# Gated cross-attention block: ScalarE scales x in place, VectorE adds the mix from PSUM, start-up loads and engine orders laid out anew

## The chip, the cores and the metric

The kernel runs on one core of one Trainium2 chip. The metric is device time in microseconds; lower is better. Before the change it is 1412.2 us, the median of three runs.

## The reference

All data are float32, and the batch has 8 samples `x[b]` of 512 rows (features) by 2048 columns. Cut to what matters:

```python
# layernorm over the 2048 columns; then windowed attention in patches of W=128 columns, 8 heads of 32 rows
q = Wq @ z + bq;  k = Wk @ z + bk;  v = Wv @ ctx + bv         # z = layernorm(x), 256 x 512 weights
s = where(mask, q.T k / sqrt(32), -1e9);  a = softmax(s)
o = gelu(a v);    x = x + tanh(g_x) * mask * (Wo @ o + bo)
# second half: a row of 2048 is one token, 64 experts with a bias of 2048 each
h = layernorm(x); p = softmax(h @ Wr.T + rb);  w = top 8 of p, all others 0
x = x + tanh(g_f) * (h * sum(w) + w @ expert_bias)
```

With `h = (x - m) * r` the last line is `x * A + B + M`: per row A = 1 + tanh(g_f) * sum(w) * r and B = -tanh(g_f) * sum(w) * r * m, while M = tanh(g_f) * (w @ expert_bias) is the mix, a matrix product.

## The kernel before

**Tiling.** A sample is a batch of the loop; it lies in SBUF as `X[b % 2]`, 4 tiles `t` of 128 rows by 2048 columns. The attention works on units of 256 columns (two windows), 8 per batch, 64 in all, numbered u. The second half runs once per batch, when unit 8b+7 is done.

**Order.** There is no planner at run time. Each engine has its own instruction stream, which the Python program writes by walking over `TICKS`; `SLOTS` gives each step a lag in slots, a unit is due every 16 slots and a batch every 128. Slots are only an order: an engine issues what is next and waits on semaphores. The steps of one unit, in the order of TensorE: `S` (scores for the maximum), `DEN`, `PV` and `R0`, `R1` of older units, `q`, `v0`, `k` projections of the next unit, `MT`, `hT0`, `hT1`, `v1`, `ST` (scores turned), `WO0`, `WO1`. Products are made of a high and a low part in fp32r, so every operand has a `_hi` written by ScalarE and a `_lo` written by GpSimd or VectorE.

**PSUM.** Seven banks form a ring (`take`): at each step of the order the bank that by the slots comes free first is taken, with the semaphore of its last reader. TensorE waits for that reader.

**The batch's end.** For batch b: `norm2` (statistics), `L` (ScalarE copies the logits), `LT` (TensorE), `c_top`, `c_exp`, `c_w` (softmax and the top 8, on VectorE and ScalarE; the last step signals `ac_v` and leaves A in `sc[:, t, 6:7]` and B in `sc[:, t, 7:8]`), `wT` (TensorE), `wt_hi`, `wt_lo`, and then 16 chunks of 512 columns: `mix` (TensorE, L463 and L464), `shift_mix` (ScalarE, L684: `xm` = mix + B, PSUM to SBUF, two buffers `xm`), `add_mix` (VectorE, L879: X = X * A + `xm`), and a store of the chunk. Between the chunks stand steps of the units that run on: `ST`, `WO0`, `WO1` and `S` on TensorE, `exp` on ScalarE, `xt0`, `xt1` (`weigh_out`, L784), `top` (L747) and `rc` (reciprocal, L768) on VectorE. GpSimd adds `xt` to X (`add_x`, L1025) meanwhile.

**Statistics of the next batch** (`input_stats`, `bn1`, L887) are 16 instructions on VectorE, from slot 64.75 of a batch with a gap of 1.25 slots. The statistics of the second norm (`stats2`, `bn2`, L793) are 4 instructions in every second unit.

**Start-up.** SyncE issues all loads: six small constants, x of batch 0 as 4 loads of 1 MB, two broadcast masks, Wq, Wk, Wv, the mask table, context, Wo, router and expert weights. VectorE waits for the constants (L904), makes the selection tiles, does the 16 statistics (L887), then the splits of Wq and Wk. ScalarE waits for Wv and copies it (L689), then `z_hi` (L603). GpSimd normalises unit 0 (`z_full`, L1001) and makes `z_lo` (L1009). Then TensorE starts. At tick `SPLIT` the splits of Wo, router and expert weights stand in the streams, and behind them on VectorE the first `k_ev` (L737).

Of the kernel before, what the change touches and what calls it, by code (L numbers as in the profile page):

```python
# [27 lines left out]
def bf16_parts(v):  # L28
# [15 lines left out]
    rows=-10.75, z32=-26, z_hi=-16.75, z_lo=-14.25, q=-11, q_ev=-9, k=-9, k_ev=-3.75, mk=-33.5, mkb=-25,  # L44

    c_hi=-15, c_lo=-10.5, v=-10.5, v_ev=-7.25, v_gap=-0.75,

    S=0.75, top=2.5, split=6, MT=9, mt_ev=8.75, ST=14.25, exp=16.5, DEN=18.25, PV=18.5, rc=19, on=21.25,

    gelu=24.25, mg=5, ot_hi=24.75, ot_lo=29, WO=30.25, WO_gap=1.5, xt=32.25, x1=35.5, bn2=40,  # L50

    h=39.5, hT=43.25, hT_gap=0.25, ht_hi=45.25, ht_lo=44.75, R=51.25,
# [12 lines left out]
V_BQ, V_SUM, V_PICK, V_ROWS, V_SEL, V_ONES3, V_IDB = 2, 4, 6, 10, 12, 13, 14  # L65
# [3 lines left out]
def gated_block_kernel(nc, x, ctx, mask, g_x, g_f, wqT, wkT, wvT, woT, bq, bk, bv, bo, wrT, rb, eb, out):  # L69
    with ExitStack() as st:  # L70
# [9 lines left out]
        def f32(ap):  # L80
# [66 lines left out]
        xm = [sb(f"xm{i}", [128, 512]) for i in range(2)]  # L147
        onef = xm[0][:, 0:128]
# [44 lines left out]
        wm_v, wT_pe, wthi_a, wtlo_v, mix_pe, xm_a, x2_v = (sem(n) for n in (  # L193
            "wm", "wT", "wthi", "wtlo", "mix", "xm", "x2"))
# [70 lines left out]
        def _(e):  # L265
# [22 lines left out]
            def v_mm(p):  # L288
# [3 lines left out]
                if p == 0:  # L292
                    e.wait_ge(v_w, 5)
# [90 lines left out]
            def project_out(u, j):  # L384
# [3 lines left out]
                if u == 0 and j == 0:  # L388
                    e.wait_ge(v_w, 7)
# [61 lines left out]
            def mix(b, t, c):  # L451
# [55 lines left out]
        def _(e):  # L507
# [60 lines left out]
            e.wait_ge(v_m, V_KEEP)  # L568
            e.dma_start(rows_d.rearrange("k p i -> p k i"), keep).then_inc(sm_rowsd, 16)
            for t in TICKS:  # L570
# [27 lines left out]
        def _(e):  # L598
# [90 lines left out]
            e.activation(wv_hi[:], wvst, ACT.Copy).then_inc(a_w, 1)  # L689
            for t in TICKS:  # L690
                if t == SPLIT:
                    e.wait_ge(v_w, 6)
# [32 lines left out]
                for i in range(16):  # L725
                    for b in batch(t, C["m_ev"] + C["m_gap"] * i):
                        shift_mix(b, i // 4, i % 4)

        @block.vector
        def _(e):  # L730
# [202 lines left out]
            e.tensor_tensor(wv_lo[:], wvst, f32(wv_hi[:]), ALU.subtract).then_inc(v_w, 1)
# [3 lines left out]
            for k, part in enumerate(bf16_parts(BIG)):  # L937
                e.tensor_scalar(keep[:, k, :], mneg, part, None, ALU.mult).then_inc(v_m, 1)
            for t in TICKS:
                if t == SPLIT:  # L940
# [10 lines left out]
                    e.wait_ge(a_w, 4)  # L951
# [41 lines left out]
        def _(e):  # L993
            def z_full(u):
# [3 lines left out]
                if u:  # L998
                    e.wait_ge(zlo_g, u)
# [115 lines left out]
```

## Time and profile before

| | |
|---|---|
| median of 3 runs | 1412.2 us (1408.51 to 1414.26) |
| profiled execution, its own time | 1407.94 us |
| its span, first to last instruction | 1406.1 us |
| granted TensorE clock, mean | 0.997 |
| busy: TensorE / VectorE / ScalarE / GpSimd | 92% / 77% / 56% / 72% |
| DMA queues | 28.7% of 16 engines, 89 GB/s |

Busy shares are averages over 64 units, 8 batch ends, the start and the tail. A matmul's duration overlaps with the next one's, so that an interval fully covered by matmuls reads as busy 20.00 of 20 us.

### The profile page before, as it was taken

Reading aid. Unit: us, or ns where it says so; the run is one execution under the profiler, and the core shown is the slowest. Engines: PE = TensorE matmul, PEld = TensorE weight load, DVE = VectorE, ACT = ScalarE, POOL = GpSimd, SP = SyncE. Lnnn points to the kernel's source line nnn. Section 1 sums busy time; section 2 is a strip of 40 time slices with the busy share of each in tenths; the row PEclk is TensorE's granted clock in tenths of the full one; section 3 lists DMA queues with packets and bytes.
Section 4 is the critical chain, followed back from the end, with each engine's and each line's share of the span. In section 5 each row is a group of like instructions: output and inputs, shape, how many; then the busy total and the mean of one; then the engine's idle time right before and its main releaser. Section 6 shows DMA issues by size and latency. Waiting matters only on the chain.

```text
span 1406.1 us, 39921 instructions
## 1 busy us (share of the span) xinstructions
PE 1300.1 (92%) x16139; PEld 1162.6 (83%) x16139; DVE 1089.4 (77%) x1949; ACT 794.1 (56%) x1430; POOL 1015.5 (72%) x988
## 2 busy tenths in 40 slices
PE   1899999899989999899998999989998999989996
PEld 1898998789977899789986899878998789978974
DVE  5468678897688867898778967889668886788666
ACT  1356655655565665655556665565556565565544
POOL 4487888578866788578885688857886678857751
PEclk9999999999999999999999999999999999999999
DMA  8331111541126211361113511154111621132003
GB/s 252 112 110 41 44 46 43 167 139 46 47 62 223 64 45 48 106 201 40 48 47 125 178 43 48 43 162 140 48 48 57 217 72 47 47 98 91 27 5 120
DMA packets 129270, 124.68 MB, mean 89 GB/s; under 512 B 12352, under 2 KB 97472, under 8 KB 128448
## 3 DMA queue, kind: packets, MB, share of 16 engines
q1 hardware_dynamic: 129088, 122.14, 28.7%
q8 instruction: 129, 2.11, 0.6%
q14 instruction: 53, 0.43, 0.1%
HBM read 88.45 MB, written 33.65 MB: 87 GB/s over the span
## 4 chain that ended last, share of the span: by engine, by line
PE 67%; DVE 20%; ACT 5%; issue 4%; DMA 2%; POOL 1%; SPq 1%; DVEq 0%; ACTq 0%; POOLq 0%
PE ring L283 7%; PE ring L284 7%; PE ring L285 7%; DVE X L879 4%; PE ring L399 4%; PE ring L358 4%; PE ring L323 4%; DVE o L768 4%; PE ring L400 4%; PE ring L401 4%; PE ring L298 3%; PE ring L299 3%; PE ring L300 3%; PE ring L367 3%; PE ring L414 3%
## 5 line engine op out<-in xcount | busy, mean ns | idle before, releaser
L283 PE MATMUL ring<-z_hi,wqk_hi 128*128 128x256 f32 x1024 | 291.3, 284 | 31.2 <-POOL z_lo L1009 31.2
L284 PE MATMUL ring<-z_hi,wqk_lo 128*128 128x256 f32 x1024 | 290.3, 283 | 0.0
L285 PE MATMUL ring<-z_lo,wqk_hi 128*128 128x256 f32 x1024 | 290.1, 283 | 0.0
L1025 POOL TENSOR_TENSOR X<-X,xt 128x512 f32<-128x512 f32 x128 | 165.9, 1300 | 141.4 <-DVE xt L784 136.3
L1041 POOL TENSOR_SCALAR hc<-X,ln 128x256 f32<-128x256 f32 x256 | 234.1, 930 | 0.5 <-POOL X L1025 0.5
L784 DVE SCALAR_TENSOR_TENSOR xt<-ring,cst,mg 128x256 f32<-128x256 f32 x256 | 112.0, 479 | 146.9 <-PE ring L401 146.9
L611 ACT ACTIVATE q<-ring,cst 128x256 f32<-128x256 f32 x64 | 30.3, 474 | 346.1 <-PE ring L285 346.1
L283 PEld LDWEIGHTS ring<-z_hi,wqk_hi 128*128 128x128 f32 x1024 | 196.8, 192 | 34.3 <-issue 31.8
L768 DVE RECIPROCAL o<-ring 128x512 f32<-128x512 f32 x64 | 214.2, 3347 | 0.2 <-PE ring L367 0.2
L1015 POOL TENSOR_TENSOR cx_lo<-cx,cx_hi 128x512 fp32r<-128x512 f32 x128 | 169.0, 1320 | 46.3 <-ACT cx_hi L619 46.3
L284 PEld LDWEIGHTS ring<-z_hi,wqk_lo 128*128 128x128 f32 x1024 | 196.8, 192 | 2.5
L285 PEld LDWEIGHTS ring<-z_lo,wqk_hi 128*128 128x128 f32 x1024 | 196.9, 192 | 0.0
L747 DVE TENSOR_REDUCE mx<-ring 128x4 f32<-128x512 f32 x256 | 158.8, 682 | 32.4 <-PE ring L323 32.3
L1009 POOL TENSOR_TENSOR z_lo<-z,z_hi 128x1024 fp32r<-128x1024 f32 x64 | 152.3, 2380 | 43.1 <-ACT z_hi L603 43.1
L399 PE MATMUL ring<-ot_hi,wo_hi 128*128 128x256 f32 x512 | 151.7, 296 | 6.7 <-ACT xm L684 5.9
L298 PE MATMUL ring<-wv_hi,cx_hi 128*128 128x256 f32 x512 | 149.7, 292 | 0.0
L1029 POOL TENSOR_TENSOR ot_lo<-o,ot_hi 128x512 fp32r<-128x512 f32 x64 | 83.1, 1299 | 89.7 <-ACT ot_hi L650 89.7
L1001 POOL TENSOR_SCALAR z<-X,ln 128x256 f32<-128x256 f32 x256 | 146.5, 585 | 0.1
L299 PE MATMUL ring<-wv_lo,cx_hi 128*128 128x256 f32 x512 | 144.5, 282 | 0.0
L400 PE MATMUL ring<-ot_hi,wo_lo 128*128 128x256 f32 x512 | 144.4, 282 | 0.0
L300 PE MATMUL ring<-wv_hi,cx_lo 128*128 128x256 f32 x512 | 144.3, 282 | 0.0
L401 PE MATMUL ring<-ot_lo,wo_hi 128*128 128x256 f32 x512 | 143.8, 281 | 0.0
(133 smaller groups left out, 3377.3 us busy)
## 6 DMA issues: line engine op xcount, KB each, us to landing
cx<-in_ctx SPq DMA_DIRECT2D x128, 256.0 KB, 2.8
out_y<-X SPq DMA_DIRECT2D x128, 256.0 KB, 2.7
X<-in_x SPq DMA_DIRECT2D x112, 256.0 KB, 5.8
mk<-in_mask SPq DMA_DIRECT2D x64, 128.0 KB, 3.2
mg<-in_mask SPq DMA_DIRECT2D x64, 128.0 KB, 3.2
X<-in_x SPq DMA_DIRECT2D x4, 1024.0 KB, 8.1
sel<-rows_d SPq DMA_DIRECT2D x256, 3.0 KB
X<-in_eb SPq DMA_DIRECT2D x2, 512.0 KB, 8.2
```

The lines of the kernel that those rows point to most:

```text
L283: e.matmul(o, wqk_hi[:, t, cols], z_hi[:, t, :], t == 0, False)
L284: e.matmul(o, wqk_lo[:, t, cols], z_hi[:, t, :], False, False)
L285: last = e.matmul(o, wqk_hi[:, t, cols], z_lo[:, t, :], False, t == DT - 1)
L298: e.matmul(o, cx_hi[:, k, :], wv_hi[:, k, :], k == 0, False)
L299: e.matmul(o, cx_hi[:, k, :], wv_lo[:, k, :], False, False)
L300: last = e.matmul(o, cx_lo[:, k, :], wv_hi[:, k, :], False, k == DT - 1)
L399: e.matmul(o, wo_hi[:, m, cols], ot_hi[:, m, :], m == 0, False)
L400: e.matmul(o, wo_lo[:, m, cols], ot_hi[:, m, :], False, False)
L401: last = e.matmul(o, wo_hi[:, m, cols], ot_lo[:, m, :], False, m == 1)
L768: e.reciprocal(o32[u % NO][:], bank("DEN", u)[:].rearrange("p (m i) -> p m i", m=2)).then_inc(rc_v, 1)
L1015: e.tensor_tensor(cx_lo[:], cx[p % NC][:], f32(cx_hi[:]), ALU.subtract).then_inc(cxlo_g, 1)
L1041: last = e.tensor_scalar(hc[u % 2][:, t, :], X[b % 2][:, t, c * U:(c + 1) * U], ln1[b % 2][:, 0, t:t + 1], None, ALU.add)
```

## The change

1. `shift_mix` and the buffers `xm` go. ScalarE gets `scale_x(b, t)`: X = X * A + B in place, one instruction of 128x2048 for each of the 4 row tiles, after `ac_v` and `h_g`. VectorE's `add_mix` becomes a `tensor_tensor` add of the mix in PSUM to X, 16 per batch as before. A mix bank is now freed by VectorE (`x2_v`) and no longer by ScalarE (`xm_a`).
2. Start-up: the mask table and x (8 loads of 512 KB, with an own semaphore `x_half` for first halves) are issued first; Wq and Wk go ahead of the broadcast masks; the six constants are issued by ScalarE's queue. ScalarE makes the high parts of Wq, Wk and Wv. VectorE normalises unit 0 and makes its `z_lo`; the mask preparation stands ahead of the statistics.
3. `SLOTS` is changed in most entries. In the stream of a unit the order on each engine stays as it was (but `mk` stands ahead of `ctx1` and `rows` ahead of `mg` in SyncE's). At the batch's end: `wT` behind `hT0`, `q_ev` ahead of `c_exp`, `ht_hi0` ahead of `wt_hi`; `scale_x` of tiles 0 and 1 stands ahead of `z_hi`, `v_ev1` and `exp`, tile 2 behind `exp`, tile 3 behind `c_hi0`. TensorE has mix 0 to 2, `ST`, mix 3 and 4, `WO0`, mix 5 to 10, `WO1`, mix 11 and 12, `S`, mix 13 to 15 (before: 0 to 3, `ST`, `WO0`, 4 to 9, `WO1`, 10 to 13, `S`, 14 and 15). The 16 statistics of the next batch start at slot 67.75 with a gap of 1.75.

```diff
-    S=0.75, top=2.5, split=6, MT=9, mt_ev=8.75, ST=14.25, exp=16.5, DEN=18.25, PV=18.5, rc=19, on=21.25,
+    S=0.5, top=2.75, split=5.75, MT=7.5, mt_ev=9, ST=14, exp=16.25, DEN=18.25, PV=19.25, rc=19, on=21,
-    norm2=29.5, L=34.75, LT=35.5, c_top=35, c_exp=36, c_w=42, wT=41.75, wt_hi=43.75, wt_lo=42.75, mix=45.25, m_gap=0.25,
-    m_ev=47.5, x2=47.25, rl=52.5, rl_gap=1,
+    norm2=29.5, L=33.75, LT=35.5, c_top=36, c_exp=35.5, c_w=41.5, wT=43.25, wt_hi=43.75, wt_lo=42.75, mix=45.25, m_gap=0.25,
+    sx=45.5, sx_gap=1.5, x2=47.25, rl=55.5, rl_gap=1,
-    x_1=0.5, x_gap=3.75, bn1=64.75, bn1_gap=1.25, norm1=95,
+    x_1=0.5, x_gap=3.75, bn1=67.75, bn1_gap=1.75, norm1=95.75,
...
-                    take(("mix", b * 16 + i), t, C["m_ev"] - C["mix"], xm_a, b * 16 + i + 1)
+                    take(("mix", b * 16 + i), t, C["x2"] - C["mix"], x2_v, b * 16 + i + 1)
...
+            e.dma_start(mT, mflat.rearrange("b (w i) -> (b w) i", i=128)).then_inc(sm_mT, 16)
             for t in range(DT):
-                e.dma_start(X[0][:, t, :], xv[0, t]).then_inc(x_in[0][t], 16)
+                e.dma_start(X[0][:, t, 0:1024], xv[0, t, :, 0:1024]).then_inc(x_half[t], 16)
+                e.dma_start(X[0][:, t, 1024:S], xv[0, t, :, 1024:S]).then_inc(x_in[0][t], 16)
...
-            def shift_mix(b, t, c):
-                i = (b * DT + t) * 4 + c
-                if i >= 2:
-                    e.wait_ge(x2_v, i - 1)
-                e.wait_ge(mix_pe, i + 1)
-                if t == 0 and c == 0:
+            def scale_x(b, t):
+                if t == 0:
                     e.wait_ge(ac_v, b + 1)
-                e.activation(xm[i % 2][:], bank("mix", i)[:], ACT.Identity, bias=sc[:, t, 7:8]).then_inc(xm_a, 1)
+                    e.wait_ge(h_g, NU * (b + 1))
+                xs = X[b % 2][:, t, :]
+                e.activation(xs, xs, ACT.Identity, bias=sc[:, t, 7:8], scale=sc[:, t, 6:7]).then_inc(sx_a, 1)
...
+            e.wait_ge(sm_wq, 16)
+            e.activation(wqk_hi[:, :, 0:E], wst[:, :, 0:E], ACT.Copy, scale=QSCALE).then_inc(a_w, 1)
+            e.wait_ge(sm_wk, 16)
+            e.activation(wqk_hi[:, :, E:2 * E], wst[:, :, E:2 * E], ACT.Copy).then_inc(a_w, 1)
             e.wait_ge(sm_wv, 16)
             e.activation(wv_hi[:], wvst, ACT.Copy).then_inc(a_w, 1)
...
-                e.wait_ge(xm_a, i + 1)
-                e.scalar_tensor_tensor(out=xs, in0=xs, scalar=sc[:, t, 6:7], in1=xm[i % 2][:], op0=ALU.mult, op1=ALU.add).then_inc(x2_v, 1)
+                if c == 0:
+                    e.wait_ge(sx_a, b * DT + t + 1)
+                e.wait_ge(mix_pe, i + 1)
+                e.tensor_tensor(xs, xs, bank("mix", i)[:], ALU.add).then_inc(x2_v, 1)
...
+            ln = ln1[0]
+            e.wait_ge(rstd1_g, 1)
+            for t in range(DT):
+                last = e.tensor_scalar(z32[:, t, :], X[0][:, t, 0:U], ln[:, 0, t:t + 1], ln[:, 2, t:t + 1], ALU.add, ALU.mult)
+            last.then_inc(z32_g, 1)
```

## Rows read from the trace of the kernel before

**Rows 1.** Busy time by engine in 20 us; columns PE, PEld, DVE, ACT, POOL, clock, DMA.

```profile
200.00:220.00 20.00, 20.00 (x259) 18.45 (x259) 13.26 (x22) 11.61 (x22) 16.83 (x18) 1.00 0.16 42
240.00:260.00 20.00, 16.60 (x144) 13.64 (x143) 15.81 (x34) 17.97 (x33) 6.25 (x4) 1.00 0.36 120
```

**Rows 2.** Timeline of VectorE, the reciprocal of five units: start, duration.

```profile
214.34 3.35 DVE L768 RECIPROCAL o<-ring 128x512 f32<-128x512 f32 x1
...
232.85 3.35 DVE L768 RECIPROCAL o<-ring 128x512 f32<-128x512 f32 x1
...
268.83 3.34 DVE L768 RECIPROCAL o<-ring 128x512 f32<-128x512 f32 x1
...
287.41 3.35 DVE L768 RECIPROCAL o<-ring 128x512 f32<-128x512 f32 x1
...
307.27 3.35 DVE L768 RECIPROCAL o<-ring 128x512 f32<-128x512 f32 x1
```

**Rows 3.** Timeline of VectorE in an ordinary unit.

```profile
209.05 0.88 DVE L784 SCALAR_TENSOR_TENSOR xt<-ring,cst,mg 128x256 f32<-128x256 f32 x2 [2.74 <-PE ring L401]
210.46 0.88 DVE L784 SCALAR_TENSOR_TENSOR xt<-ring,cst,mg 128x256 f32<-128x256 f32 x2 [0.53 <-PE ring L401]
211.94 2.48 DVE L747 TENSOR_REDUCE mx<-ring 128x4 f32<-128x512 f32 x4 [0.60 <-PE ring L323]
```

**Rows 4.** Who waited for whom, 233 to 270 us: total, times, longest.

```profile
ACT xm L684 <- DVE X L879: 6.8, 7, 2.4
...
PE ring L463 <- DVE mx L747: 2.4, 1, 2.4
```

**Rows 5.** Groups by line, whole span: busy us, mean ns, idle before.

```profile
L879 DVE SCALAR_TENSOR_TENSOR X<-X,sc,xm 128x512 f32<-128x512 f32 x128 | 114.2, 933 | 20.2 <-ACT xm L684 18.2
L684 ACT ACTIVATE xm<-ring,sc 128x512 f32<-128x512 f32 x128 | 85.5, 696 | 52.4 <-DVE X L879 48.8 <-PE ring L464 2.2 <-issue 1.4
L657 ACT ACTIVATE ht_hi<-ring 128x512 fp32r<-128x512 f32 x128 | 69.1, 597 | 10.5 <-PE ring L414 10.5
L773 DVE TENSOR_TENSOR o<-ring,o 128x512 f32<-128x512 f32 x64 | 43.8, 685 | 3.7
L464 PE MATMUL ring<-eb,wt_lo 128*128 128x512 f32 x128 | 50.6, 395 | 0.0
L697 ACT ACTIVATE eb<-X 128x2048 fp32r<-128x2048 f32 x1 | 1.9, 1900 | 0.0
```

**Rows 6.** Timeline of VectorE and of ScalarE at the first batch's end.

```profile
246.62 1.28 DVE L812 TENSOR_TENSOR ht_lo<-ring,ht_hi 128x512 fp32r<-128x512 f32 x2
...
246.06 1.06 ACT L603 ACTIVATE z_hi<-z 128x1024 fp32r<-128x1024 f32 x1
...
252.90 2.07 ACT L638 ACTIVATE P<-ring 128x512 f32<-128x512 f32 x4
```

**Rows 7.** Timeline of the start, all engines.

```profile
3.52 2.21 SPq L554 DMA_DIRECT2D X<-in_x  x4
...
8.61 9.95 DVE L887 BATCH_NORM_STATS2 bnst<-X 128x6 f32<-128x512 f32 x16 [1.07 <-DMA X<-in_x]
...
20.72 6.77 POOL L1001 TENSOR_SCALAR z<-X,ln 128x256 f32<-128x256 f32 x4
...
23.13 1.06 ACT L689 ACTIVATE wv_hi<-X 128x1024 fp32r<-128x1024 f32 x1 [17.46 <-DMA X<-in_wvT]
...
31.21 0.55 PE L283 MATMUL ring<-z_hi,wqk_hi 128*128 128x256 f32 x1 [31.21 <-POOL z_lo L1009]
```

**Rows 8.** Statistics on VectorE between 294 and 316 us (timeline).

```profile
294.82 3.05 DVE L887 BATCH_NORM_STATS2 bnst<-X 128x6 f32<-128x512 f32 x5
...
312.96 2.46 DVE L793 BATCH_NORM_STATS2 bn<-X 128x6 f32<-128x512 f32 x4
```

**Rows 9.** Timeline of ScalarE and of VectorE in the tail.

```profile
1388.07 0.60 ACT L675 ACTIVATE wt_hi<-ring 128x512 fp32r<-128x512 f32 x1 [2.93 <-PE ring L448]
...
1391.15 11.97 DVE L879 SCALAR_TENSOR_TENSOR X<-X,sc,xm 128x512 f32<-128x512 f32 x16 [1.69 <-ACT xm L684]
```

More of the change, by code:

```diff
@@ L42 @@
 SLOTS = dict(
-    rows=-10.75, z32=-26, z_hi=-16.75, z_lo=-14.25, q=-11, q_ev=-9, k=-9, k_ev=-3.75, mk=-33.5, mkb=-25,
-    c_hi=-15, c_lo=-10.5, v=-10.5, v_ev=-7.25, v_gap=-0.75,
-    S=0.75, top=2.5, split=6, MT=9, mt_ev=8.75, ST=14.25, exp=16.5, DEN=18.25, PV=18.5, rc=19, on=21.25,
-    gelu=24.25, mg=5, ot_hi=24.75, ot_lo=29, WO=30.25, WO_gap=1.5, xt=32.25, x1=35.5, bn2=40,
-    h=39.5, hT=43.25, hT_gap=0.25, ht_hi=45.25, ht_lo=44.75, R=51.25,
-    norm2=29.5, L=34.75, LT=35.5, c_top=35, c_exp=36, c_w=42, wT=41.75, wt_hi=43.75, wt_lo=42.75, mix=45.25, m_gap=0.25,
-    m_ev=47.5, x2=47.25, rl=52.5, rl_gap=1,
-    x_1=0.5, x_gap=3.75, bn1=64.75, bn1_gap=1.25, norm1=95,
+    rows=-11.75, z32=-24.75, z_hi=-16, z_lo=-16.5, q=-11.5, q_ev=-12.5, k=-9, k_ev=-3.75, mk=-38.5, mkb=-24.25,
+    c_hi=-14.5, c_lo=-10.5, v=-10, v_ev=-7, v_gap=-1,
+    S=0.5, top=2.75, split=5.75, MT=7.5, mt_ev=9, ST=14, exp=16.25, DEN=18.25, PV=19.25, rc=19, on=21,
+    gelu=24.5, mg=5, ot_hi=25.75, ot_lo=29.25, WO=30.5, WO_gap=1.5, xt=32.5, x1=35.25, bn2=40,
+    h=40.75, hT=43.25, hT_gap=0.25, ht_hi=43.75, ht_lo=44.75, R=51.25,
+    norm2=29.5, L=33.75, LT=35.5, c_top=36, c_exp=35.5, c_w=41.5, wT=43.25, wt_hi=43.75, wt_lo=42.75, mix=45.25, m_gap=0.25,
+    sx=45.5, sx_gap=1.5, x2=47.25, rl=55.5, rl_gap=1,
+    x_1=0.5, x_gap=3.75, bn1=67.75, bn1_gap=1.75, norm1=95.75,
 )
 G_IDENT, G_MXB = 2, 8
-V_BQ, V_SUM, V_PICK, V_ROWS, V_SEL, V_ONES3, V_IDB = 2, 4, 6, 10, 12, 13, 14
+V_SUM, V_PICK, V_ROWS, V_SEL, V_ONES3, V_IDB, V_BQ = 3, 5, 9, 11, 12, 13, 14
 V_KEEP, V_SW = 4, 6
@@ L146, in gated_block_kernel @@
         wt_lo = sb("wt_lo", [128, DT, 128], F32R)
-        xm = [sb(f"xm{i}", [128, 512]) for i in range(2)]
-        onef = xm[0][:, 0:128]
+        onef = sb("onef", [128, 128])
         half = sb("half", [128, DT])
@@ L170, in gated_block_kernel @@
         mflat = mask.rearrange("b o s -> (b o) s")
-        sm_small, sm_wqk, sm_wv, sm_mT, sm_wo = (sem("w_" + n) for n in ("x", "qk", "v", "mT", "o"))
+        sm_small, sm_wq, sm_wk, sm_wv, sm_mT, sm_wo = (sem("w_" + n) for n in ("x", "q", "k", "v", "mT", "o"))
         sm_rb, sm_wr, sm_eb, sm_rowsd = (sem("w_" + n) for n in ("rb", "r", "eb", "rows"))
@@ L176, in gated_block_kernel @@
             "g_set", "v_set", "v_w", "v_m", "a_w", "a_tg", "pe_set"))
+        x_half = [sem(f"xh{t}") for t in range(DT)]
         x_in = [[sem(f"x{i}_{t}") for t in range(DT)] for i in range(2)]
@@ L192, in gated_block_kernel @@
             "L", "LT", "dm", "lg", "t8", "neg", "mr", "sel", "ex", "w2", "ac"))
-        wm_v, wT_pe, wthi_a, wtlo_v, mix_pe, xm_a, x2_v = (sem(n) for n in (
-            "wm", "wT", "wthi", "wtlo", "mix", "xm", "x2"))
+        wm_v, wT_pe, wthi_a, wtlo_v, mix_pe, sx_a, x2_v = (sem(n) for n in (
+            "wm", "wT", "wthi", "wtlo", "mix", "sx", "x2"))
         TICKS = range(-32 * 8, 8 * (128 * (NB + 1) + 96))
@@ L273, in project @@
                     e.wait_ge(freed, n)
+                if u == 0:
+                    e.wait_ge(v_w, kind + 1)
                 if kind == 0:
-                    if u == 0:
-                        e.wait_ge(v_w, 4)
                     e.wait_ge(zhi_a, u + 1)
@@ L470, in _ @@
                     for k in range(SB):
-                        last = e.matmul(PR[:, 0:NX], onef, wrst[:, k, :], k == 0, k == SB - 1)
+                        last = e.matmul(PR[:, 0:NX], onef[:], wrst[:, k, :], k == 0, k == SB - 1)
                     last.then_inc(pe_set, 1)
@@ L724, in _ @@
                     w_high(b)
-                for i in range(16):
-                    for b in batch(t, C["m_ev"] + C["m_gap"] * i):
-                        shift_mix(b, i // 4, i % 4)
+                for i in range(DT):
+                    for b in batch(t, C["sx"] + C["sx_gap"] * i):
+                        scale_x(b, i)
         @block.vector
@@ L938, in _ @@
                 e.tensor_scalar(keep[:, k, :], mneg, part, None, ALU.mult).then_inc(v_m, 1)
+            for t in range(DT):
+                for r in range(4):
+                    input_stats(0, t, r)
+            input_norm(0)
+            ln = ln1[0]
+            e.wait_ge(rstd1_g, 1)
+            for t in range(DT):
+                last = e.tensor_scalar(z32[:, t, :], X[0][:, t, 0:U], ln[:, 0, t:t + 1], ln[:, 2, t:t + 1], ALU.add, ALU.mult)
+            last.then_inc(z32_g, 1)
+            e.wait_ge(a_w, 1)
+            e.scalar_tensor_tensor(out=wqk_lo[:, :, 0:E], in0=wst[:, :, 0:E], scalar=QSCALE, in1=f32(wqk_hi[:, :, 0:E]),
+                                   op0=ALU.mult, op1=ALU.subtract).then_inc(v_w, 1)
+            e.wait_ge(zhi_a, 1)
+            e.tensor_tensor(z_lo[:], z32[:], f32(z_hi[:]), ALU.subtract).then_inc(zlo_g, 1)
+            e.wait_ge(a_w, 2)
+            e.tensor_tensor(wqk_lo[:, :, E:2 * E], wst[:, :, E:2 * E], f32(wqk_hi[:, :, E:2 * E]), ALU.subtract).then_inc(v_w, 1)
+            e.wait_ge(sm_small, 96)
+            e.tensor_scalar(cst[:, BQ:BQ + 2], cst[:, BQ:BQ + 2], QSCALE, None, ALU.mult).then_inc(v_set, 1)
+            e.wait_ge(a_w, 3)
+            e.tensor_tensor(wv_lo[:], wvst, f32(wv_hi[:]), ALU.subtract).then_inc(v_w, 1)
             for t in TICKS:
```

75 lines of the change are left out of this document (29 added, 46 removed).

## The prediction

> **What bounds the kernel now.** First the busy time by stretch. In the middle of a batch TensorE is covered 20.00 of 20 us, while VectorE has 13.26, ScalarE 11.61 and GpSimd 16.83 [rows 1]. Two reciprocals then stand 18.51 us apart (232.85 - 214.34) [rows 2]: this unit is paid for by TensorE, and its order does not change, so nothing is won there. What a batch costs beyond its eight units the reciprocals show too: the unit with the batch's end takes 35.98 us (268.83 - 232.85), 17.5 too many, and a unit soon after it takes 19.86 (307.27 - 287.41), 1.35 too many [rows 2]. At the batch's end TensorE falls to 16.60 of 20 [rows 1]; a little later it waits 2.4 us in one piece for the maximum (L747), which is queued on VectorE between the chunk adds [rows 4]. Part of the 17.5 must stay, since the mix is real work: 32 matmuls at no more than 0.395 are at most 12.6 us [rows 5]. So at least 4.9 us per end can be won. VectorE and ScalarE alternate there through two small buffers: ScalarE waited 6.8 us for the add to give `xm` back [rows 4], and the add took 0.933 us in the mean, against 0.75 in the tail (11.97 / 16), where GpSimd is still [rows 5, 9].
>
> **The start.** Before, TensorE begins at 31.21. Wv lands at 23.13, but z of unit 0 is ready only at 20.72 + 6.77 = 27.5; `z_hi` and GpSimd's `z_lo` follow [rows 7]. After: x's first issue stood at 3.52 behind six constants; with one load left ahead of it, it comes 0 to 2.9 us earlier (five sixths of 3.52); I take 2.3, since the queue does not start at zero. As many bytes lie ahead of Wv as before, so it lands at 20.8. Then ScalarE copies Wv and makes `z_hi`, both 128x1024 as L689, 1.06 each: 22.9. VectorE's `z_lo` is twice the length of a 512-column step, which costs 0.62 when chained (9.95 / 16) [rows 7]: 1.24. TensorE begins at 24.2, **7.0 us earlier**. The other path is hidden: statistics from 5.5 or so to 15.5, the norm as before 2.2 (18.56 to 20.72) [rows 7], z on VectorE 4 times between 0 and 0.685 (L773, a longer instruction) [rows 5], so by 20.4 at the latest, ahead of ScalarE's 21.8. If Wv landed no earlier the gain is 4.7; if it were early enough for z to decide, with z at about 1.3, it is 9.9. Bounds: -4.7 to -9.9. The first `k_ev` stays behind the same splits and moves along. ScalarE's six issues, the copies of Wq and Wk and the late scaling of bq lie in ScalarE's 17.46 us of waiting for Wv [rows 7]; without that cover they would cost some 4 us.
>
> **The batch's end, followed through.** TensorE's stream up to `k` and VectorE's up to `c_w` are unchanged; `wT` lets `hT0` pass while it waits for the weights. On ScalarE the same three copies (`wt_hi`, `ht_hi0`, `ht_hi1`) are done in another order, and then the first `scale_x` takes the place that `z_hi` had, at 246.1 [rows 6]. Its price: a 128x2048 instruction without pointers took 1.900 (L697), and one bias pointer costs 0.10 (L684 against L657, 0.696 - 0.597), so with scale and bias 2.1 [rows 5]. It ends at 248.2. VectorE is done with `ht_lo` at 247.90 before and about 0.5 later after, because `wt_lo` waits for the later `wt_hi` [rows 6]: 248.4. So ScalarE does not hold it. From there VectorE does 15 adds, `xt0`, `xt1` and the maximum, until the last bank that the next `q` needs is free. An add from PSUM takes 0.685 (L773) alone and 0.62 chained [rows 5, 7]: 15 x 0.62 = 9.3. With 0.88 less an overlap of 0.08 for each `xt` and 2.48 for the maximum [rows 3] that is 13.4 us. Two pauses come to it. The fourth bank of `ST` is that of chunk 0, free at 249.1. From there TensorE has the rest of `ST` (as long as `S`, 211.94 - 210.46 = 1.5), two mixes (an estimate of 0.46 each: two matmuls of 0.395 that overlap) and `WO0` (210.46 - 209.05 = 1.4) [rows 3, 5]: 253.0. VectorE is through chunk 4 at 251.5: 1.5. Chunk 8 needs `scale_x` of tile 2, behind the exponentials. These end at 254.97 as before [rows 6], since tiles 0 and 1, `z_hi` and `v_ev1` are through at 251.5, so tile 2 is ready at 256.9; VectorE, with `xt0` and chunks 5 to 7 behind it, gets there at 255.8: 1.1. Then 248.4 + 13.4 + 2.6 = 264.4, and the reciprocal follows at 264.5 against 268.83 [rows 2]: **4.3 us per end**, seven times, -30. In the last batch the tail counts (below).
>
> Bounds of this term: if the adds came to 0.933 each, as L879 does beside GpSimd [rows 5], 16 x 0.31 = 5.0 would be lost again and the end be 0.7 slower; if both pauses closed, 6.9 would be won. I take the chained row, since L773 already reads one operand from PSUM and one from SBUF beside a busy GpSimd, 0.685 in the mean of 64. One rule speaks against the move. L773's 0.685 from PSUM stands against 0.65 to 0.75 for L879 with GpSimd still [rows 5, 9]. The Trainium skill ("VectorE: DVE Perf Modes", section on the TRN2 errata) gives VectorE a fixed cost of 120 cycles for an operand from PSUM and 58 for one from SBUF, an estimate of 65 ns more for each add. By that rule a batch's adds would cost 1.0 us more and the seven ends win 23 instead of 30; by the rows the full duration is known, and the sum needs no such addition.
>
> **Statistics of the next batch.** Before, 13 of the 16 fall into one unit, 5 of them in a row from 294.82 [rows 8], with `k_ev` behind them, and the unit costs 1.35 too much [rows 2]. After, 8 fall into each of two units. The first has 5 x 0.62 = 3.1 less on VectorE and fits. The second has 5 more than before and also `bn2` with 2.46, ending at 315.4 before [rows 8]: `k_ev` behind it comes up to 3.1 us later, and I take its slack at two thirds of that, so 1.0 is lost. So **0.4 us per batch** remains of the 1.35, -3; bounds 0 to -9.5. The later loads of x (55.5 for 52.5) keep their distance to the statistics, which also move by 3 slots. In SyncE's queue `mk` now waits for `k_ev` ahead of `ctx1`; that context tile is needed a unit later, so it costs nothing, and late by more than 10 us it would hold `c_hi`.
>
> **The tail.** `wt_hi` ends at 1388.67; `scale_x` of tile 0 runs to 1390.8, and the adds follow at 0.62: the last ends at 1390.8 + 9.9 = 1400.7 against 1391.15 + 11.97 = 1403.12 [rows 9]: **-2.4**. The other three `scale_x` (2.0 each) run ahead of 4 adds (2.5).
>
> **The sum.** 1407.9 - 7.0 - 30 - 3 - 2.4 = 1365.5, against the profiled execution's own time. The median of the runs is 4.3 above that execution; the after-profile may sit elsewhere in its spread, so I put the median between 1365.5 and 1369.8, at 1368.
>
> **The rivals.**
> A. More is won: VectorE's two pauses close, or the second statistics unit fits. For it: a few slots of order decide them. Against it: both follow from program order. 1407.9 - 7 - 48 - 9.5 - 2.4 = 1341, half of it 1354.
> B. The batch's end hardly moves, since banks are now freed by the engine that is shortest there, and each mix waits for VectorE: for it, the 2.4 us wait for the maximum [rows 4] stays in kind. Then only start, tail and 0 to 2 us per end: 1385 to 1402.
> C. Slower: `scale_x` in place costs far more than its row. The point is tile 3, which ends at 246.1 + 4s + 5.3; the next `q` follows it by some 4.5 us. At s = 2.1 VectorE ends later and decides. At s = 3.3 the end costs as before (269.2), at 4.2 it costs 3.5 more: 7 x 3.5 + 4.9 in the tail - 7 = +22, 1434. For it: no in-place instruction of this length is in the trace; against it: ScalarE's durations grow with the columns alone (0.597 for 512, 1.06 for 1024, 1.900 for 2048) [rows 5, 7].
> D. The start wins nothing, because Wv is bound by bytes and z waits behind three copies: 1372 to 1375 with the rest as forecast; this lies in the forecast's range.
>
> **Chances.** Forecast with D (1355 to 1385): 0.67. A (1338 to 1355): 0.15. B: 0.13. C: 0.03; all effects cancelled: 0.02. The range 1346 to 1388 leaves out half of A's and most of B's, 2 in 10. No change means within 0.5%, 7 us, about what this kernel's runs can tell. Faster 0.93 (forecast, A, nearly all of B), same 0.03, slower 0.04.
>
> **What would show it.** TensorE's first matmul near 24; the reciprocals at a batch's end 31.7 apart; `scale_x` at 2.0 to 2.1; adds at 0.62 to 0.69 with no long ones; ScalarE never waiting for VectorE's adds; a VectorE pause before `xt0` and before chunk 8; TensorE's wait for `k_ev` moved one unit on; last add at about 10 us after the first. The prediction is wrong if `scale_x` stretches, if the mix waits for banks sum to more than before, or if ordinary units leave 18.5 us.

## The result and the profile after

The kernel after takes 1391.35 us in the median of 4 runs (1388.41 to 1392.18), the kernel before 1410.97 beside it: ratio 0.986, interval 0.983 to 0.988, so 1.4% faster. The forecast was 1368. The profiled execution took 1388.41 with a span of 1386.6, against 1407.94 and 1406.1.

VectorE's 64 reciprocals cut every span into the same pieces. "Ends" are the two intervals at each of the seven batch ends, "statistics" the two that hold the next batch's statistics (each 14 intervals, 259.1 us if all took 18.51), "other" the rest. All in us:

| kernel | to first reciprocal | ends | statistics | other | last reciprocal to end | span |
|---|---|---|---|---|---|---|
| before | 67.1 | 381.2 | 270.2 | 640.4 | 47.2 | 1406.1 |
| after | 61.5 | 351.8 | 285.9 | 640.4 | 47.1 | 1386.6 |
| difference | -5.6 | -29.4 | **+15.7** | 0 | -0.1 | -19.5 |
| forecast | -7.0 | -30 | **-3** | 0 | -2.4 | -42.4 |

So 18.7 of the 22.9 us missing are the statistics. Timeline of VectorE, reciprocals of the kernel after (start, duration), the same five units as in [rows 2] and one more:

```profile
211.88 3.35 DVE L771 RECIPROCAL o<-ring 128x512 f32<-128x512 f32 x1
...
230.39 3.35 DVE L771 RECIPROCAL o<-ring 128x512 f32<-128x512 f32 x1
...
262.04 3.35 DVE L771 RECIPROCAL o<-ring 128x512 f32<-128x512 f32 x1
...
280.51 3.35 DVE L771 RECIPROCAL o<-ring 128x512 f32<-128x512 f32 x1
...
299.45 3.35 DVE L771 RECIPROCAL o<-ring 128x512 f32<-128x512 f32 x1
...
322.19 3.35 DVE L771 RECIPROCAL o<-ring 128x512 f32<-128x512 f32 x1
```

The end takes 31.65 us for 35.98. The first unit with statistics takes 18.94, but the second 22.74. Over all seven batches the second takes 21.25 (four times) or 22.7 to 22.8 (three times).

**The batch's end.** Windows of the kernel after (PE, PEld, DVE, ACT, POOL, clock, DMA), to be set beside [rows 1], then VectorE and ScalarE there, then their groups (busy us, mean ns, idle before):

```profile
240.00:260.00 20.00, 18.33 (x185) 14.45 (x189) 17.08 (x37) 16.23 (x20) 7.94 (x6) 1.00 0.56 191
```

```profile
245.98 1.87 DVE L881 TENSOR_TENSOR X<-X,ring 128x512 f32<-128x512 f32 x3
248.92 1.28 DVE L881 TENSOR_TENSOR X<-X,ring 128x512 f32<-128x512 f32 x2 [1.06 <-PE ring L464]
250.92 0.88 DVE L787 SCALAR_TENSOR_TENSOR xt<-ring,cst,mg 128x256 f32<-128x256 f32 x2 [0.72 <-PE ring L401]
...
254.29 1.89 DVE L881 TENSOR_TENSOR X<-X,ring 128x512 f32<-128x512 f32 x3 [0.71 <-ACT X L677]
...
259.05 2.48 DVE L750 TENSOR_REDUCE mx<-ring 128x4 f32<-128x512 f32 x4
```

```profile
243.62 4.07 ACT L677 ACTIVATE X<-X,sc 128x2048 f32<-128x2048 f32 x2
...
250.21 2.07 ACT L633 ACTIVATE P<-ring 128x512 f32<-128x512 f32 x4
252.14 2.12 ACT L677 ACTIVATE X<-X,sc 128x2048 f32<-128x2048 f32 x1
```

```profile
L881 DVE TENSOR_TENSOR X<-X,ring 128x512 f32<-128x512 f32 x128 | 80.9, 678 | 16.0 <-PE ring L464 9.4 <-ACT X L677 6.6
L677 ACT ACTIVATE X<-X,sc 128x2048 f32<-128x2048 f32 x32 | 66.2, 2102 | 0.0
```

The add costs 678 ns for 933 [rows 5], the scaling 2.10. VectorE has 16 adds without the long ones of before and four pauses (1.06, 0.72, 0.71 and one of 0.29), and the maximum starts at 259.05. TensorE is covered 18.33 of 20 us instead of 16.60.

**The statistics.** VectorE between two reciprocals of the kernel after, and the one instruction of GpSimd that matters:

```profile
305.25 1.68 DVE L763 CAST mxb<-mr 128x16 bf16<-128x16 f32 x1
...
307.06 0.69 DVE L891 BATCH_NORM_STATS2 bnst<-X 128x6 f32<-128x512 f32 x1
307.66 2.46 DVE L796 BATCH_NORM_STATS2 bn<-X 128x6 f32<-128x512 f32 x4
310.04 1.27 DVE L891 BATCH_NORM_STATS2 bnst<-X 128x6 f32<-128x512 f32 x2
311.22 0.86 DVE L740 SCALAR_TENSOR_TENSOR k<-ring,cst,mk 128x256 f32<-128x256 f32 x2
...
305.61 1.30 POOL L1022 TENSOR_TENSOR cx_lo<-cx,cx_hi 128x512 fp32r<-128x512 f32 x1
```

`k_ev` (L740) starts at 311.22, behind `bn2` and five statistics since the reciprocal, and behind a cast of 16 columns that took 1.68 us. In the kernel before, `k_ev` of the first and of the second unit were these:

```profile
297.80 0.85 DVE L737 SCALAR_TENSOR_TENSOR k<-ring,cst,mk 128x256 f32<-128x256 f32 x2
...
315.34 0.85 DVE L737 SCALAR_TENSOR_TENSOR k<-ring,cst,mk 128x256 f32<-128x256 f32 x2
```

Behind the reciprocal of its unit `k_ev` started after 10.39 us in the first unit (eight statistics ahead of it) and after 8.07 in the second (one statistic and `bn2`); in the kernel after it is 9.39 and 11.77. The list of waits (299 to 320 us, then the whole span) and of windows:

```profile
PE ring L354 <- DVE k L740: 2.1, 1, 2.1
...
PE ring L354 <- DVE k L740: 14.5, 7, 2.1
```

```profile
312.00:314.00 2.00, 1.86 (x48) 1.74 (x49) 2.00 (x5) 0.25 (x1) 0.82 (x1) 0.99 0.15 40
314.00:316.00 2.00, 2.00 (x11) 2.00 (x10) 1.34 (x7) 1.99 (x3) 0.51 (x1) 0.50 0.74 171
...
480.00:482.00 2.00, 2.00 (x19) 2.00 (x18) 1.93 (x9) 1.99 (x3) 0.51 (x1) 1.00 0.58 169
```

TensorE waits 2.1 us for `k` in each of seven batches; before, the same wait came to 6.1 in all, at most 0.9 each, and it stood in the first of the two units; the second had none. Behind it the granted clock was 0.50 from 314 to 316, the 1.2 GHz level, and TensorE finished 11 matmuls where it finished 19 in the same stretch of the next batch, at 2.4 GHz. That fall came in three of the seven batches and lengthens 21.25 us to 22.7.

**Start and tail.** Timeline of the kernel after at the start (as [rows 7]) and in the tail (as [rows 9]):

```profile
1.17 0.42 SPq L549 DMA_DIRECT2D X<-in_x  x1
...
6.37 1.29 DVE L891 BATCH_NORM_STATS2 bnst<-X 128x6 f32<-128x512 f32 x2 [2.06 <-DMA X<-in_x]
...
19.51 1.75 DVE L935 TENSOR_SCALAR z<-X,ln 128x256 f32<-128x256 f32 x4 [1.14 <-POOL ln L1055]
...
21.43 1.06 ACT L692 ACTIVATE wv_hi<-X 128x1024 fp32r<-128x1024 f32 x1 [1.22 <-DMA X<-in_wvT]
22.40 1.04 ACT L598 ACTIVATE z_hi<-z 128x1024 fp32r<-128x1024 f32 x1
23.47 1.23 DVE L941 TENSOR_TENSOR z_lo<-z,z_hi 128x1024 fp32r<-128x1024 f32 x1 [1.08 <-ACT z_hi L598]
24.84 0.55 PE L283 MATMUL ring<-z_hi,wqk_hi 128*128 128x256 f32 x1 [24.84 <-DVE z_lo L941]
```

```profile
1370.33 8.05 ACT L677 ACTIVATE X<-X,sc 128x2048 f32<-128x2048 f32 x4
1372.45 9.65 DVE L881 TENSOR_TENSOR X<-X,ring 128x512 f32<-128x512 f32 x16 [1.22 <-ACT X L677]
1373.16 10.18 SPq L545 DMA_DIRECT2D out_y<-X  x16
```

The adds end at 1382.1, but the span at 1386.6: 4.5 us remain, where 3.0 remained before (1406.1 - 1403.12).

### The profile page after: what moved, and what is told of

Its sections match the earlier page's. It is cut to its first block, busy times and chain, and to the rows that moved or that the text cites. A ratio compares the mean times of both kernels' runs of the same rounds, so it can differ in the third digit from the quotient of the medians.

```text
span 1386.6 us, 39734 instructions
## 1 busy us (share of the span) xinstructions
PE 1306.0 (94%) x16139; PEld 1170.6 (84%) x16139; DVE 1079.1 (78%) x1952; ACT 777.0 (56%) x1336; POOL 1001.0 (72%) x983
## 4 chain that ended last, share of the span: by engine, by line
PE 72%; DVE 20%; issue 4%; ACT 2%; SPq 1%; DMA 1%; POOL 1%; ACTq 0%; DVEq 0%; POOLq 0%
PE ring L283 6%; PE ring L284 6%; PE ring L285 6%; PE ring L399 5%; PE ring L323 5%; PE ring L358 5%; DVE o L771 5%; PE ring L400 5%; PE ring L401 4%; DVE mx L750 4%; PE ring L298 3%; PE ring L299 3%; PE ring L300 3%; PE ring L414 3%; PE ring L367 3%
## 5 line engine op out<-in xcount | busy, mean ns | idle before, releaser
L1009 POOL TENSOR_SCALAR z<-X,ln 128x256 f32<-128x256 f32 x252 | 139.1, 565 | 0.0
```

## The experiments

Eleven kernels, in the order of what they settle. Each ratio is against the kernel before on the same chip (medians 1409.9 to 1411.6); they ran on three chips, so that times of different experiments compare to about 2 us. The intervals between reciprocals are from the profiled execution of each.

**1. The old statistics in the new kernel**

```diff
-    sx=45.5, sx_gap=1.5, x2=47.25, rl=55.5, rl_gap=1,
+    sx=45.5, sx_gap=1.5, x2=47.25, rl=52.5, rl_gap=1,
-    x_1=0.5, x_gap=3.75, bn1=67.75, bn1_gap=1.75, norm1=95.75,
+    x_1=0.5, x_gap=3.75, bn1=64.75, bn1_gap=1.25, norm1=95,
```

> The changed kernel with the statistics of the next batch back at their old slots (64.75, gap 1.25; norm at 95, loads of x at 52.5). Theory S: the changed kernel is 22 us short of the forecast because the second unit with statistics grew from 18.5 to 21.2 and 22.8 us, which over seven batches costs 14.9 us (both units together). Then this kernel takes 1388.4 - 14.9 = 1373.5 in the profile, with a first unit of about 20.1 and a second of 18.5. Rival R (the in-place scaling or the new place of the loads makes VectorE late in these units, not the slots of the statistics): the two units stay at 39.5 to 41.5 together and the time at 1388.

1378.27 (1375.91 to 1381.17), ratio 0.976 [0.974, 0.978]. So the new place of the statistics costs 13 us in this kernel by the medians, and 10 by the profiled spans. The statistics' two intervals come to 275.7 instead of 285.9 and the wait for `k` to 1.5 for 2.1: it is the slots, and not rival R. But theory S had said 1373.5, with 20.1 in the first unit; it takes 20.65, with a cast of 1.68 us ahead of `k_ev` here too. Two stretches at half clock, one at a batch's end and one in these intervals, cost some 3 more.

**2. The new statistics in the old kernel**

```diff
-    x_1=0.5, x_gap=3.75, bn1=64.75, bn1_gap=1.25, norm1=95,
+    x_1=0.5, x_gap=3.75, bn1=67.75, bn1_gap=1.75, norm1=95.75,
```

> The kernel before with nothing changed but the statistics' slots (67.75, gap 1.75, norm at 95.75). Theory S: slower by 9 (no half clock) to 15 us, about 1420 in the profile, with 18.9 and 21.2 or more for the two units after a batch's end, instead of 20.1 and 18.5. Rival R: within 3 us of the kernel before.

1435.15 (1433.57 to 1439.53), ratio 1.017 [1.014, 1.019]. The new place alone makes the old kernel slower by 24 us, more than the 9 to 15 expected: its statistics intervals take 293.5 instead of 270.2, with the same wait of 2.1 for `k`, seven times, and now the half clock behind it in every batch. The clock also fell at four of the seven batch ends, which take 388.1 for 381.2.

**3. The same statistics, but none between reciprocal and split**

```diff
+BN1 = (70.0, 70.0, 71.25, 73.0, 74.75, 76.5, 78.25, 80.0, 81.75, 86.0, 86.0, 87.0, 88.75, 90.5, 92.25, 94.0)
-                    for b in due(t, C["bn1"] + C["bn1_gap"] * i, 128, NB - 1):
+                    for b in due(t, BN1[i], 128, NB - 1):
```

> The changed kernel with the two statistics that stand between the reciprocal and the split of the maximum moved behind the split, in both units. As many statistics stand ahead of k_ev as before the move. Theory C (a part of the loss is that the split's cast, at 1.68 us instead of 0.42, waits for GpSimd, which it meets only because it comes 1.2 us later): the cast is back at 0.2 to 0.45, the wait of TensorE for k_ev falls from 2.1 to about 0.8 and the half clock after it goes: 1388.4 - 7 x 1.3 - 3 x 1.5 = about 1375. Theory N (only the number of statistics ahead of k_ev counts): 1388.

1381.69 (1378.52 to 1384.26), ratio 0.978 [0.976, 0.980]. VectorE of this kernel:

```profile
302.20 0.42 DVE L766 CAST mxb<-mr 128x16 bf16<-128x16 f32 x1
...
308.34 0.85 DVE L743 SCALAR_TENSOR_TENSOR k<-ring,cst,mk 128x256 f32<-128x256 f32 x2
```

The cast is short again, and the two units take 18.51 and 20.51 for 18.94 and 21.25 where the clock stays up. Theory C had hoped for more: TensorE was to wait 0.8 us for `k` and keep its clock, but it still waits 1.8, and the clock falls in four of seven batches. `k_ev` comes 11.04 us behind the reciprocal instead of 11.77, since the smaller steps around the cast grew a little. So undoing this meeting is worth 0.43 + 0.74 us a batch, 8.2 in all; 6.6 of it show (285.9 - 279.3), because the clock fell once more often. What is left comes with the number of instructions ahead of `k_ev`. The split also stands 1.2 us earlier here, so this is the worth of both together.

**4 and 5. The statistics in VectorE's gaps, ahead of `xt` and behind `k_ev`**

```diff
+BN1 = (70, 71, 72, 73, 77.5, 77.75, 78, 78.25, 81, 82.5, 90, 91, 93.5, 93.75, 94, 94.25)   # 4
+BN1 = (70, 71, 72, 73, 74, 77.5, 77.75, 78, 78.25, 81, 82.5, 90, 91, 93.5, 93.75, 94)      # 5
```

> The changed kernel with the 16 statistics put where VectorE is idle in the trace: 4 ahead of k_ev in the unit without the second norm's statistics, 4 behind ht_lo, 1 between the two xt, 1 ahead of the maximum, 2 ahead of k_ev in the next unit and 4 behind its ht_lo. Theory S: no unit is longer than about 18.7, so the two units give 37.2 instead of 40.1 to 41.6 and the whole about 1388.4 - 7 x 3.0 - 3 x 1.5 = 1363 to 1366. If VectorE is short over the two units as a whole (16 statistics, 9.9 us, do not fit) it stays above 1375.

> As the run with the statistics in VectorE's gaps, but 5 ahead of the first k_ev and 3 behind the second ht_lo (there 4 and 4, and the norm, made TensorE wait 0.6 for xt0). Theory S: the second unit falls from 19.5 to 18.5 to 18.9, the first stays at 18.5, so 1366.7 - 7 x 0.8 = about 1361 span. If VectorE is simply full over the two units, the unit stays at 19.5 or the first grows.

The first took 1369.16 (1366.57 to 1370.0), 0.969 [0.967, 0.971]; the second **1364.44** (1363.74 to 1364.73), 0.968 [0.966, 0.969], the fastest kernel of the study, 1.8% under the kernel after by the two ratios. The first is 3 us over what theory S gave, since its second unit stays at 19.5. The statistics of the second take 262.1 us, 3.0 over the 259.1 of plain units, with no half clock and, behind the start, one wait for `k` of 0.3 in the whole run. VectorE of the second, behind the first batch's end:

```profile
276.21 3.35 DVE L774 RECIPROCAL o<-ring 128x512 f32<-128x512 f32 x1
281.86 3.05 DVE L894 BATCH_NORM_STATS2 bnst<-X 128x6 f32<-128x512 f32 x5
284.84 0.85 DVE L743 SCALAR_TENSOR_TENSOR k<-ring,cst,mk 128x256 f32<-128x256 f32 x2
...
286.81 2.46 DVE L894 BATCH_NORM_STATS2 bnst<-X 128x6 f32<-128x512 f32 x4
...
294.72 3.35 DVE L774 RECIPROCAL o<-ring 128x512 f32<-128x512 f32 x1
```

These nine statistics and two more stand between two reciprocals and cost nothing (294.72 - 276.21 = 18.51). Five stand ahead of `k_ev`, which still starts 8.63 us behind the reciprocal; the rest stand behind it and `ht_lo`.

**6, 7 and 8. Scaling and orders, one without the other.** All three have the start and the statistics of before. 6 has the in-place scaling and the adds from PSUM in the old slots; 7 the new slots with the old `shift_mix`; 8 both.

```diff
+    sx=45.5, sx_gap=1.5, x2=47.25,                               # 6, 8 (for m_ev=47.5)
+    S=0.5, top=2.75, ... ST=14, exp=16.25, ... WO=30.5, xt=32.5  # 7, 8: all slots of after but bn1, norm1, rl
```

> The kernel before with the first part of the change alone: ScalarE's in-place scaling (slots 45.5, gap 1.5) and VectorE's add from PSUM; start-up, all other slots and the statistics as before. Theory P (the batch's end gains by this part, and the new orders of wT, hT, q_ev and mix add little): a batch's end at 31.8 to 32.5 instead of 36.2, the tail 2.4 shorter, so 1407.9 - 7 x 4.1 - 2.4 = about 1377. Rival O (the new orders do a good part of it): a batch's end at 33.5 to 35, 1387 to 1398.

> The kernel before with the slots of the kernel after, but for the statistics (those of before, with the reloads of x at 52.5) and with its own start and its own shift_mix through xm. Theory N: the orders at the batch's end carry the gain, since with the scaling alone the batch cost as much as before (167.2 against 167.0 us). Then the unit with the batch's end comes to about 32 us and the time to about 1384. Theory J: the gain needs both, since ScalarE and VectorE still hand each chunk over through xm, 16 times 0.93 us on VectorE, whatever the order; then the unit with the end stays at 35 to 37 and the time at 1400 to 1420.

> The kernel before with the scaling in place and with the slots of the kernel after, but for the statistics (those of before), and with the start of before: the fourth corner of the square of scaling and orders. It is the kernel with the old statistics (1378.3) without the new start, so 1378.3 plus the 5.6 to 6.4 that the start is worth: 1384 to 1385, if the parts add up. If the start were worth nothing beyond the first unit, it would be 1378. The unit with the batch's end is expected at 31.7, the one behind it at 18.5, and no half clock at the batch's end.

| | time, us | ratio | ends, us |
|---|---|---|---|
| neither (before) | 1409.9 to 1410.3 | 1 | 381.2 |
| 6: scaling alone | 1406.57 | 0.997 [0.996, 0.998] | 382.2 |
| 7: orders alone | 1437.83 | 1.018 [1.015, 1.021] | 405.1 |
| 8: both | 1381.89 | 0.979 [0.977, 0.982] | 351.8 |

Neither part wins anything at the batch's end by itself; together they win 29.4, exactly what the kernel after has. Both theories for 6 (1377, and 1387 to 1398) were wrong. For 7, that the orders carry the gain was wrong, and theory J's 1400 to 1420 was right in kind and too low. 8 came 2 to 3 us under its 1384 to 1385, with the ends as expected. All engines of kernel 6 at the first batch's end, and its windows:

```profile
260.60 2.48 DVE L744 TENSOR_REDUCE mx<-ring 128x4 f32<-128x512 f32 x4 [0.69 <-PE ring L322]
263.00 1.27 DVE L875 TENSOR_TENSOR X<-X,ring 128x512 f32<-128x512 f32 x2
...
263.73 1.94 PE L366 MATMUL ring<-P,ones 128*32 128x512 f32 x8 [2.15 <-DVE X L875]
265.81 3.36 DVE L765 RECIPROCAL o<-ring 128x512 f32<-128x512 f32 x1 [1.53 <-PE ring L366]
```

```profile
262.00:264.00 2.00, 0.27 (x4) 0.20 (x8) 2.00 (x4) 0.00 (x0) 2.00 (x4) 0.90 0.00 0
264.00:266.00 2.00, 2.00 (x20) 0.72 (x16) 0.47 (x2) 0.00 (x0) 2.00 (x3) 0.50 0.73 260
```

`DEN` (L366) waits 2.15 us for a bank that VectorE frees only with the adds behind the maximum; TensorE is busy 0.27 of 2 us and then gets half the clock, in all seven batches; the end takes 34.0 for 36.3, and the unit behind it 20.6 for 18.2. 13 adds stand ahead of the maximum in kernel 6 and 14 in kernel 8 and the kernel after, and `DEN` starts as the 14th ends: with it goes the wait. By the slots it is `top` at 2.75 for 2.5 that lets the 14th add ahead; that slot was not tried alone. In kernel 7 VectorE's adds are the slow ones:

```profile
263.78 4.11 DVE L879 SCALAR_TENSOR_TENSOR X<-X,sc,xm 128x512 f32<-128x512 f32 x3
...
263.94 1.73 POOL L1025 TENSOR_TENSOR X<-X,xt 128x512 f32<-128x512 f32 x1 [4.43 <-DVE xt L784]
```

Three adds take 4.11 us while GpSimd adds `xt`; all 128 take 986 ns in the mean. Behind them comes the maximum, and `DEN` waits for it, 18.5 us in seven batches (11.9 in the kernel before); the clock then fell at every end too. How much of the 24 us by which the ends grew is the clock's was not separated.

**9. Tile 2's scaling ahead of the exponentials** (in the fastest kernel)

```diff
-    sx=45.5, sx_gap=1.5,
+    sx=45.5, sx_gap=1.25,
```

> The fastest kernel so far (1364.4) with one change: the gap of the scaling is 1.25 slots for 1.5, which puts tile 2's scaling ahead of the exponentials on ScalarE. VectorE waited 0.7 us for it ahead of chunk 8 in each batch; if that pause is on the path, up to 0.7 a batch is won, 1359.5. Rival: the exponentials then come 2.1 us later, and with them DEN, PV and the reciprocal (VectorE reaches it 0 to 2 us later), so the batch's end grows from 31.7 to 32 to 33.5 and the time is 1366 to 1377.

1371.13 (1370.02 to 1372.03), 6.7 us slower: the rival was right. ScalarE of this kernel at the first batch's end, then the exponentials in the fastest kernel, whose timeline agrees with this one within 0.1 us up to there:

```profile
244.45 2.09 ACT L680 ACTIVATE X<-X,sc 128x2048 f32<-128x2048 f32 x1
...
247.86 2.07 ACT L636 ACTIVATE P<-ring 128x512 f32<-128x512 f32 x4
```

```profile
245.92 2.06 ACT L636 ACTIVATE P<-ring 128x512 f32<-128x512 f32 x4
```

The exponentials start 1.9 us later, the end grows from 31.8 to 32.9, and the pause it was to close had cost 0.7.

**10 and 11. The start**

```diff
             # 10: SyncE, the six constants ahead of the mask table and x (gone from ScalarE)
+            e.dma_start(cst[:, TG:TG + 1], g_x[None, :].to_broadcast([128, 1])).then_inc(sm_small, 16)
...
             # 11: VectorE no longer makes z and z_lo of unit 0; in GpSimd's loop:
-                    if u:
-                        z_full(u)
+                    z_full(u)
```

> The changed kernel with the six constants issued by SyncE again, ahead of the mask table and x. Theory W (Wv's landing decides the start, and all loads behind the constants move with them): TensorE begins at 24.84 + 2.8 = 27.6, the whole 2.8 later. Rival Z (z of unit 0 or the statistics decide): TensorE begins at no more than 26.

> The changed kernel with z and z_lo of unit 0 made by GpSimd, as before the change. Theory G: z is ready at 19.6 + 2.2 to 6.8 (beside VectorE's split of Wq and Wk), so at 22 to 26, and z_lo takes 2.4 instead of 1.23; TensorE begins at 26.0 to 30.5. If it begins at 25.5 or earlier, moving unit 0 to VectorE was worth nothing and only the order of the loads counts.

Each put TensorE's first matmul back from 24.84 to 26.99 and 26.95, and the first reciprocal from 61.5 to 64.1 and 63.6. For 10 that is 2.15 of the 2.8 that theory W gave (Wv's copy and z both came 2.15 later); for 11 it lies in the range of theory G. One run each (1389.48 and 1392.31): their whole times lie within 2 us of the kernel after and decide nothing.

## Why the prediction was wrong, point by point

**The statistics: the step that failed.** "`k_ev` behind it comes up to 3.1 us later, and I take its slack at two thirds of that, so 1.0 is lost. So 0.4 us per batch remains of the 1.35, -3; bounds 0 to -9.5." It cost 15.7 us instead of winning 3. The mechanism was the right one: TensorE's wait for `k_ev` did move one unit on, as the prediction says at its end. Its size was wrong. Set beside each other, without the intervals in which the clock fell:

| unit | `k_ev` behind its reciprocal, us | interval above 18.51, us |
|---|---|---|
| before, second | 8.07 | 0.00 |
| experiment 5, first; 3, first | 8.63; 8.66 | 0.00 |
| after, first | 9.39 | 0.43 |
| before, first | 10.39 to 11.02 | 1.35 to 1.98 |
| experiment 3, second | 11.04 | 2.00 |
| experiment 1, first | 11.18 | 2.14 |
| after, second | 11.77 | 2.74 |

Up to about 9.0 us behind the reciprocal (11.77 - 2.74 = 9.03) `k_ev` is free, and each microsecond beyond it is paid in full. (In the second units of experiments 4 and 5, 9.26 and 9.22 with 1.0 and 0.4 above, `xt` comes late as well.) So the step breaks into three sizes:

- The slack was taken, not read: 2.1 us, where it was 1.0 (9.03 - 8.07). The kernel before could have told: its first unit paid 1.35 at 10.39.
- The delay was 3.70 us (11.77 - 8.07) and not 3.1. Four more statistics ahead of `k_ev` are 2.4 of it (by the rows 9 and 7 statistics fall into the two units, not 8 and 8); most of the rest is the cast that met GpSimd. 14 of the 64 casts of L763 took over 1 us, two in each batch but the last, and each ended 0.03 us behind the end of GpSimd's `cx_lo` (above: 305.61 + 1.30 = 306.91 and 306.93); before, 2 of 64 did. The first unit, said to fit, lost 0.43 with such a cast ahead of its `k_ev`. Lost per batch: 3.17 for a forecast of 1.0, 22.2 in seven.
- The clock had no term. The wait of 2.1 us was followed by the 1.2 GHz level in three of seven batches, 1.5 us each: 4.5.

These sum to 26.7 of the 26.8 that the statistics cost over plain units, where the kernel before paid 11.1. The bounds named no loss at all, though the text itself had counted five more instructions and `bn2` ahead of `k_ev`; that made the range too narrow on the slow side. The kernel after and experiments 1, 3, 4 and 5 show the cause by changing it in steps: 26.8, 16.6, 20.2, 7.0 and 3.0 us over plain units. Experiment 5 also shows that rival A's best case, the statistics for nearly nothing, was there to be had, but by another order.

**The batch's end: right, -29.4 for -30.** Reciprocals 31.7 apart, `scale_x` at 2.1 and adds in groups of 0.62 to 0.64 came as followed through. The pauses did not all: 1.5 ahead of `xt0` and 1.1 ahead of chunk 8 were forecast, and 1.06 ahead of chunk 3, 0.72, 0.71 and a last one of 0.29 came, so that the sums of 2.6 and 2.8 agree partly by luck. What the text did not know is that this sum holds only for the order it followed: rival B (it hardly moves, since banks are freed late) is what the scaling does in the old order (experiment 6). Rival C fell with 2.10 us for the scaling. The pause at chunk 8 is not free to close (experiment 9).

**The long adds.** In the kernel before, 107 of the 128 adds took 0.75 us in the mean, as in the tail, and 21, three in each batch but the last, took over 1 us, up to 2.0; each of the 21 ended 0.54 to 0.55 us behind the end of a GpSimd instruction. In kernel 7 all 28 long ones did so too. `shift_mix`'s add reads X and `xm`, both in SBUF. The new one reads PSUM and never took more than 0.69 beside the same GpSimd. It is also another instruction, and which of the two differences counts was not tried apart. The Trainium skill ("SBUF — State Buffer", section on the two separate sides) says that a VectorE instruction with two SBUF inputs, when the GpSimd one reads SBUF too, or in one of its two-port modes, and a GpSimd instruction exclude one another for a whole instruction; the long adds and the ends of the casts agree. The rule weighed in the prediction ("VectorE: DVE Perf Modes", TRN2 errata, of the Trainium skill), 65 ns more for an operand from PSUM, does not show: the adds cost 678 ns in the mean, less than the 0.75 of the old ones that met nothing, and the ends won 29.4, not 23.

**The start: right in kind.** TensorE began at 24.84 for a forecast of 24.2, since Wv landed at 21.43 instead of 20.8. Undone alone, the constants' new place costs 2.15 of the 6.4 us (experiment 10) and VectorE's making z 2.1 (experiment 11). The two were not undone together, so they need not add, and the order of the loads and the splits was not taken apart. z was ready at 21.3, later than the 20.4 said to be the latest, but still ahead of Wv's copy, which ScalarE began at 21.43. Rival D fell. Only 5.6 of the 6.4 reached the first reciprocal.

**The tail: the adds right, the end not.** The adds take 9.65 us for 11.97, as forecast, but the text let the span end with them. The stores now have to keep up: issues and median us to landing, before and then after, from 1355 us on:

```profile
out_y<-X SPq DMA_DIRECT2D x16, 256.0 KB, 2.6
```

```profile
out_y<-X SPq DMA_DIRECT2D x16, 256.0 KB, 3.5
```

1.5 of the 2.3 us go there: the 16 stores are 4.2 MB, and at the 390 to 400 GB/s that the DMA row shows at its highest they need 10.6 us, about as long as the adds. That the stores' rate sets the end was not tried by itself. The rest went to half clock in the tail (kernel 8 without it: 46.0 us behind the last reciprocal for 47.1).

**Do the parts add up?** From before to 8 (scaling and orders) it is -28.0, from 8 to experiment 1 (the start) -3.6, from there to the kernel after (the statistics) +13.1. A chain of differences ends at the measured time whatever the parts do, so this is an account and not a check. Checks are that the ends take 351.8 with the new start and without it, which they pass, and that the statistics' move costs the same in both kernels, which it does not: 24 us in the old one and 13 in the new, with more falls of the clock in the old. The start's smaller share in the chain (3.6 for 6.4) holds experiment 1's two falls of the clock.

## What to carry to other kernels

When background work on an engine is moved, list what stands behind it on that engine and read from the waits who already waits for it: a unit that already waits for it shows where the slack ends, and every instruction beyond that point is paid in full. The same 16 instructions cost 27 us in one place and 3 in another, while the gain at the batch's end needed both halves of the change: the cheaper add gave nothing until a bank came free ahead of a long reduction. And when the last compute gets shorter, look at the stores that drain behind it.

## What the hardware showed unasked

- A cast of 128x16 took 1.68 us instead of 0.17 to 0.42 because it met a GpSimd instruction; when that one ended, not the cast's own size, set it.
- TensorE's granted clock fell to 0.50 behind waits of 1.8 to 2.2 us, but not behind all: in 3 of 7 batches of the kernel after at 2.1, in 7 of 7 of experiment 2 at 2.1 and of kernel 6 at 2.15, in 4 of 7 of experiment 3 at 1.8; at the ends of the kernel before, waits of 2.0 to 2.4 had no fall behind them. What decides between the like cases stays open.
